# Second cross attention: the context normalised by ScalarE, the running maximum in SBUF, and two PSUM banks for the ring of fills

## The reference, cut to what matters

```python
x = layernorm(x, gamma_media, beta_media)
latents = layernorm(latents, gamma_lat, beta_lat)
kv = jnp.concatenate((x, latents * kv_gate), axis=1)
q = (latents @ Wq).reshape(b, n, HEADS, DIM_HEAD)
k = (kv @ Wk).reshape(b, f + n, HEADS, DIM_HEAD)
v = (kv @ Wv).reshape(b, f + n, HEADS, DIM_HEAD)
sim = jnp.einsum('bqhd,bkhd->bhqk', q * SCALE, k)
sim = sim - jax.lax.stop_gradient(jnp.max(sim, axis=-1, keepdims=True))
sim = jnp.where(valid_full[:, None, None, :], sim, NEG_INF)
attn = jax.nn.softmax(sim, axis=-1)
out = jnp.einsum('bhqk,bkhd->bqhd', attn, v).reshape(b, n, HEADS * DIM_HEAD)
return out @ Wout
```

## Time and profile before

| | |
|---|---|
| median of 3 runs | 2505.41 us (2494.01 to 2506.86) |
| the profiled execution, its time | 2506.49 us |
| its span, first to last instruction | 2504.7 us |
| PE busy | 2048.3 us (82%) |
| DVE busy | 1663.0 us (66%) |
| ACT busy | 1011.3 us (40%) |
| POOL busy | 1016.6 us (41%) |
| the second cross attention | from 999.8 us to about 2148 us |

### The profile page before, as it was taken

How to read it: one execution, slowest core, us unless ns; L and a number is a source line. 1 busy time by engine, 2 the same in 40 slices (tenths; PEclk the granted TensorE clock), 3 DMA queues, 4 the chain that set the end, 5 groups by cost and what they waited for, 6 DMA issues and landing times. The chain is left out here.

```text
span 2504.7 us, 35270 instructions
## 1 busy us (share of the span) xinstructions
PE 2048.3 (82%) x12728; PEld 1418.6 (57%) x12728; DVE 1663.0 (66%) x2539; ACT 1011.3 (40%) x1662; POOL 1016.6 (41%) x720
## 2 busy tenths in 40 slices
PE   7888857785999944687889888997989997499993
PEld 4555646673344433455556555665656664499992
DVE  5687743343679997489778887888778886422223
ACT  3333210001222210465666566754766674133332
POOL 2232221221344443055456645754566664122221
PEclk9999968897999976789999899998999998699996
DMA  3110044201000000200000000000000000351113
GB/s 143 36 36 20 12 171 158 76 31 59 1 0 0 1 0 3 84 1 1 12 17 1 9 1 27 1 1 9 1 1 1 9 1 1 142 202 35 39 37 109
DMA packets 36455, 93.26 MB, mean 37 GB/s; under 512 B 5160, under 2 KB 24124, under 8 KB 31679
## 3 DMA queue, kind: packets, MB, share of 16 engines
q1 hardware_dynamic: 30206, 74.72, 8.3%
q0 software_dynamic: 6080, 16.29, 1.9%
HBM read 76.56 MB, written 14.44 MB: 36 GB/s over the span
## 5 line engine op out<-in xcount | busy, mean ns | idle before, releaser
L1893 POOL TENSOR_TENSOR x_total<-x_total,x_pt 128x1024 f32<-128x1024 f32 x186 | 438.9, 2360 | 196.9 <-ACT x_pt L1952 180.7
L1973 ACT ACTIVATE x_pt<-PS,x_maskf 128x512 f32<-128x512 f32 x544 | 332.3, 687 | 181.8 <-PE PS L2241 181.4
L2055 DVE TENSOR_TENSOR PS<-x_pt,PS 128x512 f32<-128x512 f32 x480 | 333.2, 694 | 73.7 <-ACT x_pt L1973 36.5
L2212 PE MATMUL PS<-x_pt,x_vs 128*64 128x256 f32 x2176 | 287.9, 406 | 78.3 <-ACT x_pt L1952 72.4
L2073 DVE TENSOR_TENSOR x_pt<-x_pt,PS 128x1024 f32<-128x1024 f32 x320 | 320.5, 1052 | 0.7 <-PE PS L2259 0.7
L1952 ACT ACTIVATE x_pt<-x_pt 128x1536 f32<-128x1536 f32 (+1 forms) x160 | 266.1, 1664 | 50.7 <-DVE x_pt L2073 50.4
L2241 PE MATMUL PS<-x_qs,x_ks 64*128 64x256 f32 x2176 | 281.9, 395 | 1.5 <-ACT x_pt L1973 1.5
L2212 PEld LDWEIGHTS PS<-x_pt,x_vs 128*64 128x64 f32 x2176 | 154.3, 144 | 206.9 <-ACT x_pt L1952 78.4
L1131 PEld LDWEIGHTS PS<-m_xT,m_own 128*128 128x128 f32 x1984 | 235.3, 195 | 9.4 <-DVE m_own L1207 6.4
L1131 PE MATMUL PS<-m_xT,m_own 128*128 128x128 f32 x1984 | 236.3, 278 | 5.1 <-DVE m_own L1207 5.1
L2241 PEld LDWEIGHTS PS<-x_qs,x_ks 64*128 64x128 f32 x2176 | 199.5, 189 | 65.3 <-issue 39.8
(11 more groups left out here) (267 smaller groups left out, 2936.4 us busy)
## 6 DMA issues: line engine op xcount, KB each, us to landing
f_w<-in_L_ffn_w SPq DMA_DIRECT2D x32, 1024.0 KB, 6.9
a_ctxT<-in_ctxT SPq DMA_DIRECT2D x8, 800.5 KB, 4.3
f_w<-ys SPq DMA_DIRECT2D x12, 512.0 KB, 6.4
x_cx<-in_ctx SPq DMA_DIRECT2D x4, 1536.0 KB
l_w<-in_L_attn_w SPq DMA_DIRECT2D x6, 512.0 KB, 6.5
a_xT<-in_xT SPq DMA_DIRECT2D x4, 512.0 KB, 5.2
X<-in_x SPq DMA_DIRECT2D x1, 2048.0 KB, 10.8
xr<-a_xn SPq DMA_DIRECT2D x16, 128.0 KB, 1.7
```

What stands on the lines that cost most here:

```text
L1893: ins = nc.gpsimd.tensor_tensor(total2[:], first, tile[:, 2 * k + 2:2 * k + 4, :], ALU.add)
L1973: nc.scalar.activation(pt[:, s % 2, t, :].rearrange("p (h n) -> p h n", h=2), PS[:, first:first + 2, half], ACT.Identity, bias=maskf[:, b ...
L2055: ins = nc.vector.tensor_tensor(acc, tile, acc, ALU.max)
L2212: mm = nc.tensor.matmul(PS[h * HDX:(h + 1) * HDX, AVB, 0:QN], vs[:, p % 2, t, h * HDX:(h + 1) * HDX], pt[:, u % 2, t, h * QN:(h + 1) * QN] ...
```

## The change

It makes three edits in `layer1_cross`.

- The running maximum is kept in the SBUF tile `most` for all 17 steps; the bank ACC is gone. The wait on `t_done` moves from the last step to the first.
- Normalising the context of batches 1 to 3 and the gate of all batches move from VectorE to ScalarE. ScalarE computes x * rs + shift, so GpSimd also makes `shift` = -mean * rs, with two more small instructions for each batch. Normalising batch 0 stays on VectorE. The gate now follows the last N move of the batch, in slot 6 instead of slot 7.
- Bank 5 joins the ring: RB and RB + 1 in turn, four banks for the early fills instead of three, and a fill waits for the fill before last.

```diff
-    RB, ACC, AVB, MB = 4, 5, 6, 7
+    RB, AVB, MB = 4, 6, 7
...
-        EARLY_BANKS = (RB, AVB, MB)
+        EARLY_BANKS = (RB, RB + 1, AVB, MB)
...
-            return PS[:, EARLY_BANKS[n % 3] if n < EARLY_USES else RB, :]
+            return PS[:, EARLY_BANKS[n % 4] if n < EARLY_USES else RB + n % 2, :]
...
-            return n - 3 if n < EARLY_USES else n - 1
+            if n < EARLY_USES:
+                return [n - 4] if n >= 4 else []
+            return range(EARLY_USES - 4, EARLY_USES) if n == EARLY_USES else [n - 2] if n >= EARLY_USES + 2 else []
...
+                nc.gpsimd.tensor_scalar(nmu[:], mv[:, :, 0], -1.0, None, ALU.mult).then_inc(negated, 1)
                 pool.wait_ge(eps_added, b + 1)
+                if b >= 1:
+                    pool.wait_ge(ln_ready, b * NS)
                 nc.gpsimd.tensor_tensor(rs[:], ve[:], g["mhalf"][:].to_broadcast([P, NS]), ALU.pow).then_inc(rs_ready, 1)
+                pool.wait_ge(rs_ready, b + 1)
+                pool.wait_ge(negated, b + 1)
+                nc.gpsimd.tensor_tensor(shift[:], nmu[:], rs[:], ALU.mult).then_inc(shift_ready, 1)
...
+                if use[0] == "N" and use == last_turn(use[1]):
+                    gate(use[1])
+
+            def gate(b):
+                act.wait_ge(moved, MOVED[last_turn(b)])
+                for k in range(KD):
+                    ins = nc.scalar.activation(kvT[:, b % 2, k, S2:KEYS], latT[:, k, :], ACT.Copy, scale=cols[:, 4 * KD:4 * KD + 1])
+                ins.then_inc(gated, 1)
+
+            def normalise(b, i):
+                src, dst, np_ = source(b, i)
+                if i == 0:
+                    act.wait_ge(shift_ready, b + 1)
+                nc.scalar.activation(dst, src, ACT.Identity, bias=shift[0:np_, i:i + 1], scale=rs[0:np_, i:i + 1])\
+                    .then_inc(ln_ready, 1)
...
-                tile, acc = pt[:, u % 2, t, :], PS[:, ACC, :]
+                tile = pt[:, u % 2, t, :]
                 if n >= 1:
                     dve.wait_ge(s_most, n)
                 if t == 0:
-                    ins = nc.vector.tensor_copy(acc, tile)
-                elif t < KT - 1:
-                    ins = nc.vector.tensor_tensor(acc, tile, acc, ALU.max)
-                else:
                     if u >= 1:
                         dve.wait_ge(t_done, u)
-                    ins = nc.vector.tensor_tensor(most[:], tile, acc, ALU.max)
+                    ins = nc.vector.tensor_copy(most[:], tile)
+                elif t < KT - 1:
+                    ins = nc.vector.tensor_tensor(most[:], tile, most[:], ALU.max)
+                else:
+                    ins = nc.vector.tensor_tensor(most[:], tile, most[:], ALU.max)
...
-            dve.wait_ge(w_loaded, 16 * 6)
-            gate(0)
...
-                        if i in (3, 4):
-                            at = (i - 3) * NG + gi - 1
-                            for k in (2 * at, 2 * at + 1):
-                                if 0 <= k < NS:
-                                    normalise(b + 1, k)
-                        if i == UB - 1 and gi == 0:
-                            gate(b + 1)
```

More of the change, by code:

```diff
@@ L1693, in layer1_cross @@
         bn, mv, ve, rs = sb("bn", [P, NS, 6]), sb("mv", [P, NS, 2]), sb("ve", [P, NS]), sb("rs", [P, NS])
+        nmu, shift = sb("nmu", [P, NS]), sb("shift", [P, NS])
         bn2, mv2, ve2, rs2 = sb("bn2", [P, J, 6]), sb("mv2", [P, J, 2]), sb("ve2", [P, J]), sb("rs2", [P, J])
@@ L1713, in layer1_cross @@
         stats_ready, eps_added, rs_ready, ln_ready = sem("stats_ready"), sem("eps_added"), sem("rs_ready"), sem("ln_ready")
-        gated = sem("gated")
+        negated, shift_ready, gated = sem("negated"), sem("shift_ready"), sem("gated")
         chain = sem("chain")
@@ L1977, in _ @@
                         exponent(s - 1, gi - 1)
+                    if exists(s) and s // UB + 1 < B and s % UB in (3, 4):
+                        at = (s % UB - 3) * NG + gi - 1
+                        for k in (2 * at, 2 * at + 1):
+                            if 0 <= k < NS:
+                                normalise(s // UB + 1, k)
         @block.vector
@@ L1994, in stats @@
                     dve.wait_ge(cx_loaded, 32 * (b + 1))
+                    if b >= 1:
+                        dve.wait_ge(shift_ready, b)
                 return token(nc.vector.bn_stats(bn[0:np_, i, :], src))
@@ L2009, in normalise @@
                     .then_inc(ln_ready, 1)
[L2011 to L2015, removed]
             def taken(use):
@@ L2141, in fill @@
                 n = USE[use]
-                if before(n) >= 0:
-                    released(pe, BY_NUMBER[before(n)])
+                for earlier in before(n):
+                    released(pe, BY_NUMBER[earlier])
                 out = bank(use)
```

## The result

The changed kernel takes 2717.72 us (median of 4 runs, 2708.90 to 2721.89) against 2505.68 us of the kernel before measured beside it: a ratio of 1.0853, 95% interval 1.0811 to 1.0895. It is 212 us slower; 2702 was forecast. The profiled execution spans 2716.0 us, 211.3 more than before.

The account below looks back on a forecast made before the run. TensorE was taken to set the pace in the second cross attention, VectorE following closely. +270 (maximum in SBUF) - 40 (normalising) - 15 (gate) - 20 (second bank) = +195, giving 2702 us; range 2590 to 2815.

Parts of the forecast that it names:

- The lock and its price: Maximum steps with two SBUF inputs and GpSimd's SBUF adds exclude each other for a whole instruction: +270 us.
- The replay of one slot: Short slot of the second cross attention, instruction by instruction: 35.8 for 27.05 us, 8.7 more, saved gaps included.
- the first rival: Steady slots: more adds fall into maximum groups and TensorE may get less clock; 2782, up to 2899 us; chance 0.10.
- One slot for 31: The 8.7 us of one short slot was taken for all 31 steady slots, V slots too: +270 us.
- the signs named: Changed profile: maximum steps mean 1.2 to 1.3 us, slots 35 to 39 us, last maximum step TensorE's largest wait.
- The saved gaps: Between maximum steps in SBUF, gaps of 0.03 for 0.10: some 16 links lose 0.07, 1.1 us a slot.
- Normalising and gate, 40 and 15: Moved to ScalarE: normalising saves about 40 us in batches 1 to 3, the gate 15 us of TensorE's waits.
- The second bank, 20: Ring of two banks: about 20 of some 27 us of TensorE's waits on ring moves go.
- Faster (2431): A maximum into its own SBUF input does not meet GpSimd, so no price: 2431, down to 2397 us; chance 0.05.
- the overlap only (2601): Only maximum steps under an add today are delayed: 5.5 x 31 = 170, less 75: 2601 us; chance 0.08.
- The harder lock (2782): Late VectorE lets more adds hit maximum groups: two more hits at half price, 11.3 a slot, 2782 us; chance 0.10.

Follow-up runs that it names:

- the one-wait run: Kernel with only normalising and gate on ScalarE (2436 us), maximum steps of groups 2 to 5 waiting once for their whole group's score moves: 2456.21 us.

## Why the prediction was right

- **The lock and its price.** The step that decided was the reading of the earlier trace rows: two SBUF inputs on VectorE and an SBUF add on GpSimd exclude each other for a whole instruction. The prices taken from there held to about 0.01 us where VectorE waits: a blocked step ends 0.55 behind the add and a round takes 2.76 (2049.03 to 2051.79 in the short slot, 2.77 replayed); an add ends 2.21 and 2.26 behind the step (2.22). Forecast for the part: +270; measured alone: +261. The rule of the Trainium skill that was named beside it ("SBUF — State Buffer", Who interferes with whom) agrees: with the long adds cut, the long steps fall from 188 to 15.
- **The replay of one slot.** It said 35.8 for 27.05; the slot takes 36.95. The waits came to 8.8 us instead of the 9.8 replayed, and the copy is 0.27 shorter. Three small things were missed and more than outweigh that: the gaps stayed (1.1, next point), the first copy comes 2.74 us after the reduction's start instead of 1.79, and the reduction 1.09 instead of 0.75 after the last step. The last two lie in TensorE's turn of the slot, at a lower granted clock: 0.72 from 2060 to 2066, where it was 1.00 from 1906 to 1910, and the four transposes of the maximum take 1.00 us instead of 0.66. The V slot takes 39.24, 10.4 more instead of 8.7, at 0.85 instead of 1.00. That TensorE would be less clocked stood only in the first rival.
- **One slot for 31: in part luck.** The price came from the shortest slot of all and was taken 31 times. With the maximum alone in SBUF the mean loss is 8.5 us a slot, but single slots lose from 0.4 to 13.1. The replay's number of hits, six or seven, fits the mean of the changed kernel, 188 in 31 slots; why the other slots average out at its price is not shown. Of the signs named, slots of 35 to 39 us held for 8 of 31: they are 36.95 to 47.8, 40.4 in the mean. And the last maximum step was not TensorE's largest wait.
- **The saved gaps: wrong.** The step "a chain of steps with all operands in SBUF has a gap of 0.03, so each link loses 0.07" took the gap between L1580 and L1583 for a property of SBUF. The gaps of 0.104 stayed in SBUF, and the runs with one wait show 0.03 in PSUM; the difference lies in which wait is a separate instruction. The figures of the Trainium skill set beside it ("VectorE: DVE Perf Modes", the section on the TRN2 errata) seemed to agree by their 62 cycles; no run here shows such a difference for the maximum steps, which have a median of 0.693 with both inputs in SBUF and a mean of 0.695 with one in PSUM, with gaps of 0.104 in both.
- **Normalising and gate, 40 and 15.** As a part alone 69, of which the gate 21 and normalising 48: too small by a fifth. In the changed kernel it was only 39 (or 31 with one bank): too large. One thing that was missed is the fourth slot of each batch. GpSimd works in order, and its remaining adds stand behind the deviations, which wait for VectorE's last statistics. With VectorE late, GpSimd idles 8.96 us for them until 1454.35 in the slot that takes 46.3, and 6.23 until 2099.81 in the last batch (3.19 before), whose slot takes 47.8 although it never had any normalising (32.53 plus 8.7 gives 41). The adds then run into the first group, where VectorE's copy takes 2.29 us and the three maxima behind it 6.00:

```profile
2099.81 0.60 POOL L1887 TENSOR_SCALAR x_ve<-x_mv 128x4 f32<-128x4 f32 x1 [6.23 <-DVE x_mv L2062]
2101.98 7.32 POOL L1902 TENSOR_TENSOR x_total<-x_total,x_pt 128x1024 f32<-128x1024 f32 x3
...
2104.81 2.29 DVE L2080 COPY x_most<-x_pt 128x512 f32<-128x512 f32 x1 [1.47 <-ACT x_pt L1997]
2107.20 6.00 DVE L2082 TENSOR_TENSOR x_most<-x_pt,x_most 128x512 f32<-128x512 f32 x3
```

- **The second bank, 20.** 18 measured.
- **The sum.** Forecast: +270 - 55 - 20 = +195. Measured, one part after the other: maximum +261, moves to ScalarE -31, second bank -18, together +212. So the lock was 9 us too dear, the relief of VectorE 24 too large, and the forecast came out 17 low. Had the relief been measured alone first, at 69, the sum would have been +174: the parts don't add up, since the relief is worth less in slots that the lock makes long. That the two errors partly cancel is luck; the size of the lock is not.
- **The rivals.** Faster (2431) and the overlap only (2601) are out. The harder lock (2782) named the two things that were underestimated, late adds and the clock, but not at that size.

## What to carry to other kernels

Before an operand of a VectorE step is moved from PSUM to SBUF, count its SBUF inputs: with the second one the step here waited for GpSimd, up to nearly a whole instruction of the other at each meeting. One tensor input is not always safe either: a copy from SBUF to SBUF (0.427 us alone, up to 2.286 in the changed kernel) and the normalising from SBUF to SBUF of the kernel before waited too, while the subtraction with its second input in PSUM did not. The price can be read from any stage that has such a pair already, and here a replay of one slot by these prices gave the part to within 9 us of 261, though single slots are far from it. If the pair can't be avoided, cut the neighbour's instructions short. And measure the parts of such a change one by one: here the moves to ScalarE alone give 69 us with the maximum in PSUM, while the second bank can't be had beside it, since it is the maximum's own.

## What the runs showed of the hardware that I had not expected

- When the wait for the VectorE instruction just before is a separate semaphore instruction, the gap is 0.104 us, in PSUM and in SBUF alike; otherwise it is 0.034, with one wait (in PSUM, the one-wait run) and with two (in SBUF).
- An SBUF to SBUF copy of 512 fp32 columns takes 0.427 us where the copy into PSUM took 0.695, but it too waits for GpSimd (up to 2.29).
- More GpSimd instructions at half the length, each of them 1.47 us in the mean where the short adds of the earlier trace rows took 1.28, gave back half of the loss: 105 of 212 us.
- A blocked maximum step ends 0.54 to 0.56 us behind the end of GpSimd's instruction, in all 188 cases of the changed kernel.
